# A four-layer graph network on one core: group counts of TensorE moved from the last matmul onto a drain

## The reference

```python
h = relu(layernorm(x)); x = x + segment_sum(h[src] @ weight[edge_type_16], dst)           # layer 0
h = relu(layernorm(x)); x = x + elu(mean(h[src] by dst) @ W_l.T + b_l + h @ W_r.T)         # layer 1
h = relu(layernorm(x)); m = silu(cat(h[src], h[dst], edge_attr) @ w1 + b1) @ w2 + b2       # layer 2
x = x + layernorm(h + silu(cat(h, segment_sum(m, dst)) @ w3 + b3) @ w4 + b4)
h = relu(layernorm(x)); score = (h[dst] @ Wq) . (h[src] @ Wk1 + rel @ Wk2 + rule @ Wk3)    # layer 3
x = x + relu(layernorm(segment_sum(softmax_by_dst(score) * (h[src] @ W_r[edge_type_8]), dst) + bias))
```

## Time and profile before

| | us |
|---|---|
| median of 2 runs | 2661.4 |
| the runs | 2665.6 and 2657.2 |
| span of the profiled execution, first to last instruction | 2690.8 |
| PE busy in it | 1523.2 |
| POOL busy | 1543.2 |
| DVE busy | 1051.5 |
| ACT busy | 487.3 |

### The profile page before, as it was taken

The page is one execution under the profiler, slowest core; times in us unless marked ns, Lnnn a source line. Parts: engine busy times, 40 slices in busy tenths (PEclk is TensorE's granted clock), DMA queues, the critical chain, the costliest instruction groups (busy, mean ns, idle before and its releaser), DMA issues.

```text
span 2690.8 us, 27765 instructions
## 1 busy us (share of the span) xinstructions
PE 1523.2 (57%) x8443; PEld 1343.0 (50%) x8443; DVE 1051.5 (39%) x2213; ACT 487.3 (18%) x1153; POOL 1543.2 (57%) x1509
## 2 busy tenths in 40 slices
PE   5545332424478888765376667659553536445564
PEld 2224332424367777765376666658332325435554
DVE  4446110111556565633122222223524634334467
ACT  2100000000356666501000000001211111001020
POOL 5447766764667777735566666662344556665620
PEclk8656555555677777766555655657656766666677
DMA  6432122120111111103122222222341212222210
GB/s 199 130 110 86 24 84 58 36 61 16 30 31 36 34 37 34 33 12 65 37 52 50 57 51 51 58 51 44 110 162 52 65 54 66 61 55 68 58 39 13
DMA packets 159861, 159.26 MB, mean 59 GB/s; under 512 B 108361, under 2 KB 111993, under 8 KB 158748
## 3 DMA queue, kind: packets, MB, share of 16 engines
q1 hardware_dynamic: 111372, 89.07, 11.7%
q0 software_dynamic: 48352, 68.42, 11.5%
HBM read 118.71 MB, written 46.06 MB: 61 GB/s over the span
## 4 chain that ended last, share of the span: by engine, by line
another core or an unknown queue 30%; DVE 21%; PE 17%; issue 16%; POOL 10%; DVEq 2%; ACT 1%; DMA 1%; SPq 1%; ACTq 0%; POOLq 0%
POOL flat L583 10%; DVE flat L824 7%; PE ps L1353 4%; DVE oh L785 2%; DVE oh L1043 2%; PE ps L1388 2%; PE ps L1511 2%; DVE msg L1034 2%; DVEq L333 1%; PE ps L1341 1%; DVE msg L960 1%; DVE ohT L791 1%; PE ps L1325 1%; PE ps L1509 1%
## 5 line engine op out<-in xcount | busy, mean ns | idle before, releaser
L583 POOL DMA_INDIRECT flat<-table,flat x1061 | 1122.8, 1058 | 639.7 <-issue 314.7
L1388 PE MATMUL ps<-flat,oh 128*128 x1664 | 328.9, 380 | 368.1 <-DVE oh L785 255.3
L785 DVE TENSOR_TENSOR oh<-iota_n,drel 128x1024 f32<-128x1024 f32 x156 | 190.1, 1223 | 867.8 <-remote 605.0
L1388 PEld LDWEIGHTS ps<-flat,oh 128*128 128x128 f32 x1664 | 314.3, 291 | 394.7 <-issue 392.7
L583 POOL DMA_INDIRECT flat<-table,tile_idx x359 | 346.7, 966 | 267.9 <-DVE base L1037 140.2
L1353 PE MATMUL ps<-msg,oh 128*128 128x64 f32 x832 | 173.3, 393 | 156.5 <-ACT msg L1209 135.4
L1353 PEld LDWEIGHTS ps<-msg,oh 128*128 128x128 f32 x832 | 166.6, 304 | 160.4 <-issue 160.4
L1366 PE MATMUL ps<-uvT,flat 128*128 128x192 bf16 x2200 | 229.3, 275 | 25.7 <-ACT flat L1191 17.2
L1366 PEld LDWEIGHTS ps<-uvT,flat 128*128 128x128 bf16 x2200 | 219.8, 112 | 34.6 <-issue 29.3
L1576 PE MATMUL ps<-qn,ohT 128*128 x832 | 159.0, 349 | 124.9 <-issue 104.0
L1511 PEld LDWEIGHTS ps<-uvT,ohT 128*128 128x128 f32 x832 | 178.3, 291 | 64.3 <-issue 48.9
(11 more groups left out here) (320 smaller groups left out, 1481.9 us busy)
## 6 DMA issues: line engine op xcount, KB each, us to landing
table<-flat SPq DMA_DIRECT2D x52, 512.0 KB
drow<-slot_node SPq DMA_DIRECT2D x104, 256.0 KB
flat<-table,flat POOLq DMA_INDIRECT x1061
flat<-edge_attr_by_slot SPq DMA_DIRECT2D x52, 128.0 KB
edge_attr_padded<-edge_attr SPq DMA_DIRECT2D x1, 6250.0 KB
flat<-table,tile_idx POOLq DMA_INDIRECT x359
flat<-tile_source SPq DMA_DIRECT2D x22, 256.0 KB
edge_attr_by_slot<-flat SPq DMA_DIRECT2D x2, 2048.0 KB
```

The source lines that it names most:

```text
L583: nc.gpsimd.indirect_dma_start(dest(t % PLACES), None, table, at_).then_inc(tile_gat[k % TRING], 16)
L785: V.tensor_tensor(oh[:, b], iota_n[:].unsqueeze(1).broadcast_to([P, SG, P]), drel[:, g * SG:(g + 1) * SG].unsqueeze(2).broadcast_to([P, SG ...
L1388: last = T.matmul(acc[:, bass.ds(n[j] * pitch + shift, width)], oh[:, b % 2, j, :], got[:, bass.ds(place[j], width)], start=False, stop=Tr ...
```

## The change

At six places the semaphore increment is taken off the last matmul of a group and put on a drain of PE that follows it. The drain is issued in order, finishes when all older PE instructions are complete, and then adds one. Counts of transposes, of `pick`, of the node products and of the softmax steps stay on their matmuls.

```diff
             def sum_into_nodes(b, n, rows_):
                 for j in range(SG):
                     last = T.matmul(acc[:, bass.ds(n[j] * D, D)], oh[:, b, j, :], rows_[:, j, :], start=False, stop=True, skip_group_check=True)
-                last.then_inc(s("used"), 1)
+                pe.drain().then_inc(s("used"), 1)
...
                         last = T.matmul(acc[:, bass.ds(n[j] * pitch + shift, width)], oh[:, b % 2, j, :], got[:, bass.ds(place[j], width)],
                                         start=False, stop=True, skip_group_check=True)
-                    last.then_inc(s("used"), 1)
+                    pe.drain().then_inc(s("used"), 1)
...
                         last = T.matmul(eb[b % 2][:, j * D:(j + 1) * D], ohT[:, b % 2, j, :], v[:, bass.ds(n[j], 1), :].rearrange("p t d -> p (t d)"), start=False, stop=True, skip_group_check=True)
-                last.then_inc(s("eb_ps"), 1)
+                pe.drain().then_inc(s("eb_ps"), 1)
...
                     last = T.matmul(qr_ps[g % 2][:, j // 4, j % 4], ohT[:, b % 2, j, :], qn_room[:, bass.ds(n[j] * QR, P)], start=True, stop=True)
-                last.then_inc(s("qr_ps"), 1)
+                pe.drain().then_inc(s("qr_ps"), 1)
...
-                last.then_inc(s("used"), 1)
+                pe.drain().then_inc(s("used"), 1)
```

## The result

The changed kernel takes 2978.7 us in the median of two runs (2966.5 and 2991.0), the kernel before 2661.4: the ratio is 1.119, with a 95% interval of 1.111 to 1.127. It is slower, as forecast, but by 317 us and not by 109, and it lies outside the range that I gave. The profiled execution spans 2989.1 us, 298.3 more than the one before.

The account below looks back on a forecast made before the run. The kernel was taken as bound largely by a cycle of gather burst, PE counts held to its end, DVE, then POOL. Terms 27 + 4 + 8 + 41 + 29 = 109 us on 2661.4 gave 2770, 4.1% slower, range 2700 to 2850.

Parts of the forecast that it names:

- The bubble: Idle PE time per drain where PE has work: 0.5 us without register loads, 1.1 with one, 1.7 with two.
- The last groups of layer 3: The last 8 groups of layer 3 go from 2.55 to 3.6 us each: 9 us.
- Layer 0: Drains cost 4 us in the first 12 groups and more at the bare end: 17.5 us for the layer.
- A held completion holds the drain: In gather bursts a drain ends only when held completions end, so PE cannot run ahead; forecast case, chance 0.54.
- the rival of counts on time: A drain's count is not held in gather bursts: -230 us, +50 for bare drains, about 2480; chance 0.22.
- POOL is started again by L960, whose `eb_ps` is older, so the burst begins at the same time: Layer 2: a sum delayed by a held drain does not delay POOL's next burst of gathers.
- would come 2 to 3 us later: Layer 2: the sum L1353 starts late behind the held `edges2`; half of 2.6 us per pair entered the upper bound.
- Layer 2: 113.5 for 41: Forecast for layer 2: 8 us for the last 5 groups, 33 for the 47 others at 0.7 each.
- I count 0.4 each: Layer 1, 22 periods: drains partly fall into the hold and cost 8 us; bounds 0 and 37.
- The clock ... I add nothing: PE's granted clock: busier PE was granted more, so bubbles promise no gain there; 0 us added.
- 29 were counted for all of layer 3: Layer 3: 9 us for the last 8 groups, 20 for the 52 others at 0.4 each.
- dearer drain: Rival: each drain costs over 1 us by itself, or layers 2 and 3 fall to one group per burst; 2880, chance 0.06.

Follow-up runs that it names:

- f8: Changed kernel with the next group's register loads put ahead of the drain: 2266.7 us, ratio 1.015 to the kernel before, counts on time.
- e14: Changed kernel, DVE waiting at every second group of layer 2 until POOL's last allowed gather landed: 2881 to 2937 us, ratio 1.078 to the kernel before, late.
- e15: Changed kernel, PE waiting between the `edges2` drain and the sum for that gather's landing, layer 2: 2965.7 us, ratio 1.108 to the kernel before, late.
- e17: Repeat of e15 (changed kernel, landing wait on PE in layer 2) in an on-time set: 2514.9 us, ratio 1.128 to the kernel before.
- f5: The changed kernel itself, run again where counts are on time: 2317.9 us, ratio 1.041 to the kernel before.
- f6: The kernel before, unedited, run for its trace where counts are on time: 2229.9 us.
- e2: Changed kernel with only the 208 drains that count `used`; `eb_ps` and `qr_ps` back on matmuls: 2286.2 us, ratio 1.028 to the kernel before.
- f7: Changed kernel with each of the 312 drains doubled, the count on the second: 2331.4 us, ratio 1.044 to the kernel before.
- e11: Changed kernel, PE waiting at every second group of layer 2, behind the `edges2` drain, for POOL's count of issued gathers: 2363.5 us against 2229.1 before.
- e12: Changed kernel with seven matmuls of zeros behind each step's last drain in layer 3's final quarter: 2319.1 us, ratio 1.040 to the kernel before.

## Why the prediction was right and wrong

- **The bubble, right.** 1.7 us where PE is bare with two loads: 1.65 of idle and 1.86 more distance. The last groups of layer 3 went from 2.55 to 3.69 (3.6 forecast). Its parts are now measured, where counts are on time: 0.36 us of idle time are left with the loads ahead of the drain, and 1.29 go with the two loads behind it (f8). Layer 0 was forecast at 17.5 and got 7.6 and 3.1: only four groups stood bare at its end.
- **A held completion holds the drain, right.** Late, 12 of `pick`'s matmuls come one or a few at a time to the end of a burst, PE restarts 2.7 us after POOL's last gather, and `edges2` is not run ahead. The Trainium skill's page "PSUM — Partial Sum Buffer", section "Engine vs sequencer instructions", has a drain wait for the engine to be idle; the drain between 1597.5 and 1606.26 agrees. So the rival of counts on time fell, as far as a drain was to bring them. What counts on time are worth was seen all the same, through another cause: 432 us, not the 230 of that rival.
- **The step that failed: "POOL is started again by L960, whose `eb_ps` is older, so the burst begins at the same time".** The input of L960 is older, but L960 stands behind L785 in DVE's queue, and L785 waits for `used`. As long as the sum runs ahead of the held drain this costs nothing (e14: stop 4.1 us). Where the sum is behind it, the stop is 7.8 to 9.1 (17 of 20 in the changed kernel, e15, and e17 by hand). I had even noted that L1353 "would come 2 to 3 us later", and did not follow its count through DVE's queue to POOL. Layer 2: 113.5 for 41. This place is 91 of it by the pair e15 and e14, and the 22 that are left are what the drains cost in this layer where counts are on time (21.6).
- **"I count 0.4 each" in layer 1** failed alike: 92.2 for 21.5. PE was 2 us early for the release, which looked like cover; a group that slips past the point where completions slow pays the rest of the burst and its own 3.7 us. Here the position is shown by the rows, and no run moved it on purpose. That it is fragile shows in runs whose layer 1 is the same code: from its first `pick` to its last sum 527 us in e15, 568 in the changed kernel, 580 in e14, with stops of POOL of 2 to 4 us in e15 and mostly 7.2 in e14. What decides between them stays open.
- **"The clock ... I add nothing"** failed: of the 34 us more in the last quarter of layer 3, 15.5 are idle time and 18.5 longer matmuls at a granted 0.64 for 0.87; on time it is 13 and 20 of 33. f5's first three steps take 14.1 us where f6's take 5.9 to 8.8. 29 were counted for all of layer 3. The rule that I had read from the earlier trace rows, the busier the higher the clock, did not even order its own rows: 0.55 stands at 66% busy and 0.61 at 47%. The drains lowered the clock in this stage, but not by the length of their gaps alone (e2). The rest of its 85 us, where counts are late, is in the earlier quarters, whose pairs of groups take up to 30.7 us; no run splits it further.
- **The range.** The condition of the runs, late or on time, moves the price from 89 to 317 us. The forecast of 109 lies near the price without the hold's extra, which is no merit: it was made for the late condition. The "dearer drain" rival (half of the upper bounds, 2880) had the size nearest, but for a reason, a drain of over 1 us by itself, that f7 refutes.

## What to carry to other kernels

When an instruction makes an engine wait for its own past, list what stands behind it in its queue, and then follow each count to the end: not only to the instruction that reads it, but through that engine's queue to whatever is behind the reader. In layer 2 here a held drain added nothing to POOL's stop with one group ahead of it, and 4 to 5 us with the same group behind it. If a drain must be, put the sequencer's own work (register loads) ahead of it: that gave back 51 of 89 us where counts were on time.

## What the runs showed of the hardware

- The same kernel took 2229 us in four sets on three chips and 2661 to 2681 us in two, with nothing in the program changed. In the slower ones PE's completions during POOL's gather bursts come late, up to the burst's end (DVE's L785 at 1390.82 for matmuls that ended at 1382.4); in the others DVE starts 0.04 us after the matmul it waits for, amid the gathers. Chip number 5 showed both. What causes it, no run here tells.
- A drain of PE that finds it empty costs under 0.1 us (f7). One behind a group costs 0.36 us of idle time (f8), plus 0.59 to 0.65 for each register load behind it. All this is where no completion is held; where they are, drains behind `edges2` took 4.4 us in the median.
- An increment that POOL gives behind its gathers came about 4 us before the last of them started (e11). For the end of a burst the landing is the event to wait for.
- With drains in the last quarter of layer 3 (gaps of 3.0 us in a step) the granted clock of that stretch was 0.61 and 0.64 where it was 0.87, and a group of 16 matmuls took 3.67 us in the first steps where it took about 1.9. Gaps of 2.6 us in a step left it at 0.84 (e2), and filling the largest gap gave 0.77 over the first four steps (e12).
